# Copies set behind the next turn's seed, TensorE's products placed by the next unit's columns, and the gate's bias put into the bank by ScalarE

## The reference

```python
pe = softmax(posembed @ pos_w + pos_b)
y = _moe_mlp(hidden_states, sg_w, su_w, sd_w)                      # the shared expert
for i in range(16):
    gate_feature = hidden_states * pe[i] @ gate_w + gate_b         # 625 x 768
    gate_weight, gate_idx = top_k(gate_feature, 384)               # sorted, over the features
    gate_weight = softmax(gate_weight)
    gathered = take_along_axis(hidden_states, gate_idx)
    y = y + _moe_mlp(gathered * gate_weight, eg_w[i], eu_w[i], ed_w[i])
return silu(layernorm(y) @ m1_w + m1_b) @ m2_w + m2_b
```

## Time and profile before

| | |
|---|---|
| median of 3 runs | 6864.56 us (6859.67, 6864.56, 6872.76) |
| the profiled execution's own time | 6858.79 us |
| its span, first to last instruction | 6857.0 us, TensorE's mean granted clock 0.954 |
| busy over the span | PE 5903.5 us (86%), DVE 5292.2 (77%), ACT 2698.2 (39%), POOL 3698.7 (54%) |
| ends of turn 0, 1, 2, 3 (start of `keep_keys`) | 1536.17, 1873.03, 2201.14, 2535.35 us |
| end of turn 15 | 6526.54 us |

### The profile page before, as it was taken

One profiled execution on the slowest core, in us unless ns is written; L12 is line 12 of the kernel. 1 busy time (PEld: TensorE's weight loads), 2 busy tenths in 40 slices (PEclk: granted clock), 3 DMA queues, 4 the chain that ended last, 5 costly groups with the idle time before them and its releaser, 6 DMA issues. The chain is left out here.

```text
span 6857.0 us, 74245 instructions
## 1 busy us (share of the span) xinstructions
PE 5903.5 (86%) x16985; PEld 3088.7 (45%) x16985; DVE 5292.2 (77%) x6633; ACT 2698.2 (39%) x4297; POOL 3698.7 (54%) x3692
## 2 busy tenths in 40 slices
PE   7979989889887988888888888888888888888988
PEld 5545545444444444444444444444444444444554
DVE  3012002599999999999999999999999999998950
ACT  0000000344544445454545454545454545444531
POOL 2324015366665656565656565656565656565740
PEclk9989999999999999999999999999999999999999
DMA  3356247000000000000000000000000000001001
GB/s 90 103 142 172 101 120 193 30 21 14 14 14 15 14 14 14 14 14 14 14 14 14 14 14 14 14 28 0 28 0 28 14 14 14 14 17 46 14 35 50
DMA packets 118072, 260.91 MB, mean 38 GB/s; under 512 B 39164, under 2 KB 49922, under 8 KB 117682
## 3 DMA queue, kind: packets, MB, share of 16 engines
q1 hardware_dynamic: 70322, 180.18, 7.4%
q0 software_dynamic: 47360, 77.17, 5.0%
HBM read 222.43 MB, written 34.58 MB: 37 GB/s over the span
## 5 line engine op out<-in xcount | busy, mean ns | idle before, releaser
L1194 PE MATMUL mask_ps<-key,neg_ident 125*125 125x480 f32 (+7 forms) x4128 | 1883.1, 575 | 519.8 <-DVE key L1569 514.4
L1453 ACT COPY mask_ps<-key 125x960 f32<-125x960 f32 (+7 forms) x1152 | 955.1, 829 | 1769.8 <-DVE pay L1609 1103.0
L1296 POOL TENSOR_TENSOR pay<-pay_side,pay 125x480 int32<-125x480 int32 (+5 forms) x1120 | 1102.0, 984 | 879.3 <-DVE pay L1592 872.6
L1194 PEld LDWEIGHTS mask_ps<-key,neg_ident 125*125 125x125 f32 x4128 | 731.4, 192 | 1404.9 <-DVE key L1569 929.7
L1288 POOL TENSOR_TENSOR pay_side<-pay 125x480 int32<-125x480 int32 (+5 forms) x1120 | 1098.1, 981 | 486.6 <-DVE pay L1609 351.9
L1592 DVE COPY_PREDICATED pay<-mask_ps,pay 125x960 f32<-125x960 int32 (+6 forms) x1120 | 1236.7, 1104 | 86.2 <-PE mask_ps L1194 63.1
L1559 DVE TENSOR_TENSOR key<-mask_ps,key 125x960 f32<-125x960 f32 (+6 forms) x1120 | 1089.1, 972 | 51.5 <-PE mask_ps L1194 34.6
L1569 DVE TENSOR_TENSOR key<-mask_ps,key 125x960 f32<-125x960 f32 (+6 forms) x1120 | 1088.9, 972 | 0.0
L1194 PE MATMUL mask_ps<-key_top,neg_ident 125*125 125x480 f32 (+3 forms) x1472 | 618.4, 549 | 237.2 <-DVE key_top L1569 223.4
L1609 DVE COPY_PREDICATED pay<-mask_ps,pay_side 125x480 f32<-125x480 int32 (+5 forms) x1120 | 709.6, 634 | 4.8 <-DVE pay L1592 2.9
L1130 PE MATMUL slot_ps<-gate_w,xs 128*125 128x384 f32 x1920 | 709.3, 507 | 0.0
(11 more groups left out here) (184 smaller groups left out, 5939.2 us busy)
## 6 DMA issues: line engine op xcount, KB each, us to landing
w_rel<-L_gnn_W SPq DMA_DIRECT2D x16, 2304.0 KB, 23.3
w_exp<-L_ffn_ed_w SPq DMA_DIRECT2D x16, 2304.0 KB, 8.3
messages_dram<-y_out SPq DMA_DIRECT2D x16, 1875.0 KB
w_exp<-L_ffn_eg_w SPq DMA_DIRECT2D x16, 1152.0 KB, 5.3
w_exp<-L_ffn_eu_w SPq DMA_DIRECT2D x16, 1152.0 KB, 7.8
root_w<-L_gnn_root SPq DMA_DIRECT2D x2, 2304.0 KB
w_exp<-L_ffn_sg_w SPq DMA_DIRECT2D x4, 1152.0 KB, 5.8
w_exp<-L_ffn_su_w SPq DMA_DIRECT2D x4, 1152.0 KB, 8.6
```

Source lines behind the costliest of these rows:

```text
L1194: last = pe.matmul(mask, neg_ident[0:TP, 0:TP], operand, start=False, stop=True, skip_group_check=True)
L1296: pool.tensor_tensor(second, shares(pay_was(turn, u), turn, u)[1].bitcast(I32), first, ALU.subtract).then_inc(pays_taken, 1)
L1453: act.copy(seed_of(turn, u), compared(turn, u)[0]).then_inc(seeded, 1)
```

## The change

Four things are changed, three of them named in the title:

1. **Presets.** All three now stand behind the next turn's `seed(1)`, in unit 0. `preset(0)` waits for the kept copies, `preset(1)` and `preset(2)` for all payloads of the turn before. `keep_keys` moves from behind unit 91's `copy_pays` to ahead of it.
2. **Spread.** `beside` adds up the columns of unit u + 1 in place of those of unit u, for PE, ACT and POOL alike.
3. **Bias.** For the gate products of experts 1 to 15 and tiles 0 to 3 (8 of 10 per expert, 120 in all) the one-row matmul goes. A copy of the bias over all partitions, `bias_rows`, is made once; ACT copies a half of it (125x384) into the bank once it has emptied that bank of the product two places earlier, and PE waits for `bias_set`. Expert 0's gate and tile 4's keep the matmul. Ahead of the first transposes of the experts' part PE fills the two banks by four matmuls, ACT copies the bias out twice, and PE waits for that.
4. `third_rest`, a buffer that `keep_pays` fills, now lies in a part of `u_feat`.

```diff
         def beside(turn, products, lag, first, last):
             passing, ends = 0, []
             for u in range(first, last):
-                passing += columns(compared(turn, u)[0])
+                passing += columns(compared(turn, u + 1)[0])
                 ends.append(passing)
...
-        third_rest = sb("third_rest", [TP, RUN * NT // 2])
+        third_rest = u_feat[:, :, :].rearrange("p k c -> p (k c)")[0:TP, D:D + RUN * NT // 2]
...
+        def is_set(e, t):
+            return t < AHEAD and not (isinstance(e, int) and e == 0)
...
                     room(n)
-                    pe.matmul(slot, ones[0:1, 0:TP], gate_b[0:1, cols], start=True, stop=False)
+                    if is_set(e, t):
+                        pe.wait_ge(bias_set, (e - 1) * NEARLY + (2 * t + half + 1))
+                    else:
+                        pe.matmul(slot, ones[0:1, 0:TP], gate_b[0:1, cols], start=True, stop=False)
...
+            pe.wait_ge(gate_loaded, 16 * (2 * BLK + 1))
+            for half in range(2):
+                pe.matmul(slots[half], ident[0:TP, :], h_mixed[:, 0:BANK], start=True, stop=True)
+                last = pe.matmul(slots[half][0:TP, 0:HALF], ones[0:1, 0:TP], gate_b[0:1, half * HALF:(half + 1) * HALF],
+                                 start=True, stop=True)
+            last.then_inc(slots_primed, 1)
+            pe.wait_ge(bias_ready, 2)
...
+            def set_bias(n, bank, half):
+                act.wait_ge(emptied, n - 1)
+                act.copy(slots[bank][0:TP, 0:HALF], bias_rows[:, half * HALF:(half + 1) * HALF]).then_inc(bias_set, 1)
...
                     if turn is REGULAR and u == 0:
+                        act.wait_ge(kept, i * NKEPT)
+                        preset(0)
                         act.wait_ge(pays_done, turn.done("units", i, 0))
-                        preset(NSET - 1)
+                        for q in range(1, NSET):
+                            preset(q)
+                    if turn.units[u] == (JOIN, 0, 2):
+                        keep_keys()
                     copy_pays(turn, i, u)
...
-                    if turn.units[u] == (JOIN, 0, 2):
-                        keep_keys()
                     if turn.units[u] == (JOIN, 1, 2):
                         keep_pays()
-                    if turn.units[u] == (JOIN, 1, 2) and following is REGULAR:
-                        act.wait_ge(kept, i * NKEPT + NKEPT)
-                        preset(0)
-                        act.wait_ge(pays_done, turn.done("units", i, u))
-                        preset(1)
```

More of the change, by code:

```diff
@@ L1375, in mixed, with with_biases, both @@
                     act.copy(up_act[:, pair_n % 2, 0:count], slots[1][:, 0:count]).then_inc(emptied, 1)
+            def set_bias(n, bank, half):
+                act.wait_ge(emptied, n - 1)
+                act.copy(slots[bank][0:TP, 0:HALF], bias_rows[:, half * HALF:(half + 1) * HALF]).then_inc(bias_set, 1)
+            def with_biases(products):
+                if products[0][0] is take_feat:
+                    for n, bank, _, _, half in [args for _, args, _ in products[0:2]]:
+                        set_bias(n, bank, half)
+                todo = []
+                for n, (work, args, parts) in enumerate(products):
+                    later = products[n + 2] if n + 2 < len(products) else None
+                    if later is not None and later[0] is take_feat and is_set(*later[1][2:4]):
+                        todo.append((both, ((work, args), (set_bias, (later[1][0], later[1][1], later[1][4]))), parts))
+                    else:
+                        todo.append((work, args, parts))
+                return todo
+            def both(*works):
+                do(works)
             def take_feat(n, bank, e, t, half):
@@ L1500, in sort @@
                         scale(i - 1, u - SCALE)
-                    if turn.units[u] == (JOIN, 0, 2):
-                        keep_keys()
                     if turn.units[u] == (JOIN, 1, 2):
                         keep_pays()
-                    if turn.units[u] == (JOIN, 1, 2) and following is REGULAR:
-                        act.wait_ge(kept, i * NKEPT + NKEPT)
-                        preset(0)
-                        act.wait_ge(pays_done, turn.done("units", i, u))
-                        preset(1)
                     do(todo.get(u, []))
+            act.wait_ge(slots_primed, 1)
+            for half in range(2):
+                act.copy(bias_rows[:, half * HALF:(half + 1) * HALF], slots[half][0:TP, 0:HALF]).then_inc(bias_ready, 1)
+            act.wait_ge(bias_ready, 2)
             for n in range(NHALF):
@@ L1522, in _ @@
             seed(OPENING, 0, 0)
-            sort(OPENING, 0, beside(OPENING, gate_products(1, PIECES) + piece(0, OPEN_BASE), 1, 1, OPENING.n - 6), REGULAR)
+            sort(OPENING, 0, beside(OPENING, with_biases(gate_products(1, PIECES) + piece(0, OPEN_BASE)), 1, 1,
+                                    OPENING.n - 6), REGULAR)
             sort(REGULAR, 1, beside_all(
-                REGULAR, gate_products(2, SECOND_BASE, range(AHEAD)) + piece(1, SECOND_BASE + NEARLY),
-                expert_in(0, SECOND_IN) + gate_products(2, SECOND_IN + NIN, range(AHEAD, NT)), 1), REGULAR)
+                REGULAR, with_biases(gate_products(2, SECOND_BASE, range(AHEAD)) + piece(1, SECOND_BASE + NEARLY)),
+                with_biases(expert_in(0, SECOND_IN) + gate_products(2, SECOND_IN + NIN, range(AHEAD, NT))), 1), REGULAR)
             with act.Fori(2, NEXP - 1) as i:
```

13 lines of the change are left out of this document (7 added, 6 removed).

## The result

| | before | after |
|---|---|---|
| median on one chip | 6862.11 us (4 runs, 6849.04 to 6872.76) | 6796.97 us (4 runs, 6784.21 to 6808.24) |
| ratio of the times, 95% interval | | 0.9905 [0.9879, 0.9932] |
| the profiled execution, its span | 6858.79, 6857.0 us | 6784.21, 6782.4 us |
| from top key to top key, 13 intervals | 330.9 us each | 324.7 us each |

The change makes the kernel 65 us faster by the medians and 74.6 us between the two profiled executions; 45.5 us and a median of 6819 were predicted. The mark that I use from here on is the *top key* (`neg_max`, one small VectorE instruction per turn, in unit 38): it stands in the same place in every kernel.

A forecast was written before the change was run, and what follows sets the result against it. VectorE, busy 315.6 us of each 328 or 334 us turn, was taken as the bound. Terms -54.3 + 6 - 4 - 3 + 0 + 5 + 4.8 = -45.5 gave 6819 us from 6864.6, range 6790 to 6862.

The forecast's parts named there:

- the step on presets: Loop's end: VectorE's own branch back sets larger(1), so the earlier seed gains 0 there; 3 us at three unlooped places.
- payload waits for masks, 13 looped turns: Payload copies' waits for masks, turns 1873 to 6174 us: of 62.2 us, 54.3 can go, 7.9 stay at unit 86.
- clock falling in new idle places: New idle places behind units 27, 29, 31, 35 and 39 let TensorE's clock fall: 6 us lost, bounds 0 and 40.
- copies on ScalarE: Bias copies ahead of seeds at units 45 and 41 cost 0.4 us a turn: 5 us lost, bounds 0 and 26.
- presets in the loop: Twelve looped boundaries: the earlier seed gains 0 each, since VectorE's own branch decides; the other end is 20 us.
- turn 1, from first maximum to top key: Turn 1's payload waits: 4 us of 7.7 gained, since its gate products stay denser.
- presets, three unlooped boundaries: Into turns 1, 2 and 15: larger(2) comes 1.0 us earlier at each, 3 us gained.
- opening: Two more priming matmuls, two bias matmuls, two ACT copies and two handings-over before the sort: 4.8 us lost.
- turn 15 and closing: Turn 15: moving its many products gains in one unit what it loses in another: 0, within 5 us either way.
- the clock falls elsewhere: Rival: payload waits due to clock falls, 32 us, only move to other places; 6845 us, chance 0.17.
- The seed decides: Rival: at the loop's branch the seed sets larger(1), so 20 us more are gained; 6799 us, chance 0.13.
- ACT becomes late: Rival: all eight bias copies per turn delay a seed by 0.6 us, 62 us in 13 turns; 6876 us, chance 0.10.

The follow-up runs named there:

- two idle places filled: Kernel before, none of the edits, two useless matmuls of 384 columns more behind mask(28) and mask(84): ratio 0.9950 to the kernel before.
- The filler behind unit 84: Changed kernel with the presets put back, two useless matmuls of 384 columns more behind mask(84): ratio 0.9889 to the kernel before.
- a fourth: Changed kernel with bias matmuls back on TensorE, two useless matmuls more behind mask(41), (43), (57) and (84): ratio 0.9956, without them 0.9941.

## Why the prediction came out as it did

The forecast's direction and its mechanisms at most of the places held; the size was 20 us short by the medians and 29 by the profiled executions, and the step on presets was right in its cause and wrong in its sum. That the total came so near is in part luck. Edits 2 and 3 stand in the sum with -54.3 + 6 - 4 + 5 + 4.8 = -42.5, and gave 32 us without the presets (interval 20 to 44). The presets stand there with -3, and were worth 32 us alone and 33 when taken out: by far the largest miss. By stretch, the 74.6 us between the two profiled executions come about so: +8.0 ahead of the experts' part, which the change doesn't touch; +5.8 up to the first maximum; -7.7 to the first top key; -81.1 in the thirteen intervals; -7.7 in the next (turn 14 to 15); +7.0 in the last; +1.1 behind it. Term by term (the terms overlap a little and leave some out, so that they don't sum to this):

| term | predicted | measured |
|---|---|---|
| payload waits for masks, 13 looped turns | -54.3 | 62.2 to 4.9: -57 |
| clock falling in new idle places | +6 | +5: 2.3 at units 40 and 41 (3 falls), 2.9 at unit 55 (2 falls) |
| waits of 0.2 us marked issue, at full clock | none | +4: 1.2 to 5.4 |
| copies on ScalarE | +5 | -10: seeds 18.7 to 8.5 |
| payload waits for ScalarE | none | 7.1 at units 9 and 29 gone, 3.2 new elsewhere: -4 |
| presets in the loop | 0 at larger(1) | -0.5 there |
| VectorE's own busy time, 13 intervals | none | -7.5 (4102.2 to 4094.7) |
| turn 1, from first maximum to top key | -4 | -7.7 |
| presets, three unlooped boundaries | -3 | -3.3, from the old turn's last first payload copy to larger(2) |
| opening | +4.8 | +5.8 |
| turn 15 and closing | 0, within 5 | +7 from its top key on |

- **Payload waits.** The end state was forecast well. The reason was half of it. I took each wait as belonging to a unit and to the edit that works there. The single edits show that it doesn't: bias or presets alone, which leave unit 28 without a product, take its falls from 9 turns to 1 and 2, and the spread alone, which gives it one, leaves 14.6 us at unit 29 and puts 21.6 at unit 41. With nothing but two idle places filled, 37 us can be had; the 11.5 us of unit 31, at full clock, stay then and need the edits.
- **The clock term, +6.** "Four to five new ones at a quarter of it" came out near the measured value by luck of the combination. At the place behind 39, one of those named, unit 41 waits 20.0 to 21.6 us with the bias on TensorE and 1.5 in the changed kernel; the place ahead of unit 55 wasn't named.
- **ScalarE, +5.** A bias copy takes 483 ns, for the 0.5 us assumed. The step "The bias copy would put 0.45 more ahead of it" is right without the spread (9 us lost). With the spread the feature copy itself stands earlier and the seed of unit 45 waits 0.7 in place of 1.0 us. And I had overlooked the 0.4 us that larger(0) waited in each turn for its seed, 5.2 us; it stood behind the copy of the kept keys, which the first edit moves. Together the term had the wrong sign.
- **Presets at the branch.** That VectorE's branch, and not the seed, sets the loop's end is shown twice: the 2.56 us stay when the seed is 4.3 us early, and go when that loop alone is written out. The page "Advanced Engine Details and Errata" of the Trainium skill, section Control Flow Timing, has a compare-and-branch at about 108 ns; here the branch with all around it costs 2.5 to 2.9 us between the end of one instruction and the start of the next, and the measurement decides. But the sum's 3 us for the edit missed what the edit does to the clock: without it the changed kernel loses 37 us over the thirteen intervals, and waits 26.1 us at unit 86 in place of 3.2. The filler behind unit 84 takes these away with the presets still left out, so they are due to the clock. That it is the 0.4 us a turn of larger(0) which keeps the clock up, and not another shift in the edit's timing, is argued and not shown. Where the code runs on unlooped, the wait came up at another place than I had it: larger(2) has its seed in time, and first(0) waits 0.7 to 0.8 us for its mask.
- **Turn 15.** The waits for a mask at units 75 and 81 grew from 1.9 to 4.2 and from 1.4 to 3.0 us:

```profile
6379.81 1.16 DVE L1602 TENSOR_TENSOR key<-mask_ps,key 125x960 f32<-125x960 f32 x1 [4.25 <-PE mask_ps L1204]
...
6401.78 1.16 DVE L1602 TENSOR_TENSOR key<-mask_ps,key 125x960 f32<-125x960 f32 x1 [3.01 <-PE mask_ps L1204]
```

  I had written "what it loses in another" and 0. From its top key on the dense turn takes 295.5 to 300.6 us in the kernels with the spread and 293.3 to 294.4 in those without; the 3.0 us at unit 81 are in all of the former, the 4.2 at unit 75 in three of them. So the loss is 2 to 7 us, and the spread makes it.

Of the rivals, "the clock falls elsewhere" describes what the spread alone or the presets left out would have done, and not this kernel. "The seed decides" and "ACT becomes late" are refuted by the traces above.

What stays open: what of the timing makes the clock fall at one passing of the same idle place and not at another. It repeats while a turn keeps its length; that is seen in these traces, its rule is not. Nor is it known whether the spread is worth having at all: the changed kernel without it is the same within the uncertainty, and to keep it out of turn 15 alone, which by the above should give 2 to 7 us, was not tried.

## What to carry to other kernels

A wait that comes only when the granted clock falls belongs to the idle place ahead of it and to the timing of the whole loop. Changes far from it can turn it on or off: look at the granted clock in each turn before a wait is charged to the instruction next to it, and judge an edit by many executions of the whole kernel, not by the waits at its own place in one trace. If TensorE lets its clock fall in a gap of 2 us and feeds another engine that has little slack, a filler in the gap is a cheap test, and sometimes a fix: it helped in three kernels here and did nothing in a fourth, where the falls stood at other places. A branch back on the engine that bounds the loop is paid nearly in full; here it was enough to write the loop out on that engine alone.

## What the runs showed of the hardware

- The same TensorE gap of 1.98 us, with the same 1.9 us of work in the 4 us ahead, was followed by half clock in one kernel and by full clock in another; so was a gap of 0.94 us with 3.06 us of work. Two useless matmuls, 1.45 us, in a gap of 2.14 us kept the clock up there in all 13 turns.
- Turns of some kernels settle on a length to within 0.4 us for six turns and more (324.2 after, 327.7 with the bias alone and with the presets alone, though the edits differ). The presets, worth 0.4 us a turn at larger(0), change the mean from 327.5 to 324.7.
- VectorE's branch back costs 2.5 to 2.9 us from the end of one instruction to the start of the next, twelve times over, even when all that the next one needs is there.
- At the same instructions VectorE's busy time differed by 7.5 us over thirteen turns. I have no explanation for it.
- ScalarE's copy of 125x384 float32 into a PSUM bank took 483 ns (112 copies, 482 to 485), out of a bank 477.
